# Local attention and last head attention: score products of 64 columns in two halves of the array, local scores issued ahead of the turning

## The reference, cut to what matters

```python
def _L0_xattn_ref(x, cond, Wq, bq, Wk, bk, Wv, bv, Wo, bo):   # local: 8 heads of 8 channels, window 16
    q = _pointwise(Wq, bq, x)
    k = _pointwise(Wk, bk, cond)
    v = _pointwise(Wv, bv, cond)
    k = jnp.pad(k, ((0, 0), (0, 0), (pad_left, pad_right)))
    v = jnp.pad(v, ((0, 0), (0, 0), (pad_left, pad_right)))
    idx = jnp.arange(T)[:, None] + jnp.arange(W)[None, :]
    k_win = k[:, :, idx].reshape(B, H, hd, T, W)
    v_win = v[:, :, idx].reshape(B, H, hd, T, W)
    dots = jnp.einsum('bhdt,bhdtw->bhtw', qh, k_win) * scale
    attn = jax.nn.softmax(dots, axis=-1)
    out = jnp.einsum('bhtw,bhdtw->bhdt', attn, v_win)
    return _pointwise(Wo, bo, out)
...
def _L3_xattn_ref(hidden_states, cross_attention_states, ...):   # 32 heads of 128, 8 key heads
    q, k = _rmsnorm(q, q_norm_w), _rmsnorm(k, k_norm_w)
    scores = jnp.einsum('bhqd,bhkd->bhqk', q, k) * scale + attention_mask
    probs = jax.nn.softmax(scores, axis=-1)
    out = jnp.einsum('bhqk,bhkd->bhqd', probs, v)
    return out @ Wo.T
...
x = x + jnp.tanh(g_xattn[0]) * _L0_xattn_ref(_layernorm(x), ctx_4096, ...)
x = x + jnp.tanh(g_ffn[0]) * _L0_ffn_ref(...)
...
x = x + jnp.tanh(g_xattn[3]) * _L3_xattn_ref(_layernorm(x), ctx_4096, ...)
x = x + jnp.tanh(g_ffn[3]) * _L3_ffn_ref(...)
```

## Time and profile before

| | us |
|---|---|
| median of 3 runs | 3497.05 |
| lowest and highest | 3487.21, 3498.43 |
| the profiled execution, device time | 3486.49 |
| its span, first to last instruction | 3484.5 |
| local phase, first to last band addition on DVE (63 steps) | 450.3 |
| PE busy in the whole span | 3262.8 (94%) |
| granted TensorE clock, share of full speed, whole span | 0.974 |

### The profile page before, as it was taken

How to read it: one execution, slowest core, us unless ns; L and a number is a source line. 1 busy time by engine, 2 the same in 40 slices (tenths; PEclk the granted TensorE clock), 3 DMA queues, 4 the chain that set the end, 5 groups by cost and what they waited for, 6 DMA issues and landing times. The chain is left out here.

```text
span 3484.5 us, 51177 instructions
## 1 busy us (share of the span) xinstructions
PE 3262.8 (94%) x19590; PEld 2651.0 (76%) x19590; DVE 1750.7 (50%) x3665; ACT 1461.6 (42%) x3278; POOL 1106.1 (32%) x673
## 2 busy tenths in 40 slices
PE   7777779999999999999999997999999999999997
PEld 5666655788888888888875444888788878888885
DVE  4666554333443343334344366555655565555554
ACT  4444422444444444444432354444444434444443
POOL 5444413223322322332212012334333433343332
PEclk9888879999999999999999999999999999999999
DMA  2000011111211211111101202222222222222211
GB/s 101 1 1 1 1 40 49 61 67 61 73 67 61 79 61 61 67 61 61 62 27 49 106 13 73 66 68 67 79 67 62 84 61 63 76 61 67 67 43 55
DMA packets 56549, 199.67 MB, mean 57 GB/s; under 512 B 8976, under 2 KB 9744, under 8 KB 53008
## 3 DMA queue, kind: packets, MB, share of 16 engines
q1 hardware_dynamic: 56336, 196.76, 17.1%
HBM read 192.54 MB, written 4.19 MB: 56 GB/s over the span
## 5 line engine op out<-in xcount | busy, mean ns | idle before, releaser
L1731 POOL TENSOR_TENSOR h_wol<-h_ro,h_woh 128x1024 fp32r<-128x1024 f32 x128 | 313.7, 2451 | 612.1 <-ACT h_woh L1782 612.1
L1727 POOL TENSOR_TENSOR h_wql<-h_rq,h_wqh 128x1024 fp32r<-128x1024 f32 x128 | 309.0, 2414 | 508.0 <-ACT h_wqh L1777 508.0
L2223 DVE COPY h_tf<-ps 128x512 f32<-128x512 f32 (+1 forms) x256 | 142.5, 557 | 610.9 <-PE ps L2004 610.8
L2227 DVE TENSOR_TENSOR h_ol<-ps,h_oh 128x512 fp32r<-128x512 f32 x256 | 176.9, 691 | 527.0 <-ACT h_oh L1835 526.7
L141 PE MATMUL ps<-h_woh,h_oh 128*128 128x512 f32 x1024 | 427.3, 417 | 5.7 <-DVE h_ol L2227 5.6
L141 PE MATMUL ps<-h_Xh,h_wqh 128*128 128x512 f32 x1024 | 414.3, 405 | 3.0 <-ACT h_qf L1831 1.4
L143 PE MATMUL ps<-h_woh,h_ol 128*128 128x512 f32 x1024 | 404.8, 395 | 0.0
L142 PE MATMUL ps<-h_wol,h_oh 128*128 128x512 f32 x1024 | 404.2, 395 | 0.0
L143 PE MATMUL ps<-h_Xh,h_wql 128*128 128x512 f32 x1024 | 402.2, 393 | 0.0
L142 PE MATMUL ps<-h_Xl,h_wqh 128*128 128x512 f32 x1024 | 399.9, 391 | 0.0
L1885 ACT ACTIVATE h_ex<-ps,h_mx 128x128 f32<-128x128 f32 x512 | 180.9, 366 | 270.8 <-DVE h_mx L2263 270.7
(11 more groups left out here) (292 smaller groups left out, 6351.3 us busy)
## 6 DMA issues: line engine op xcount, KB each, us to landing
h_rq<-in_L_Wq SPq DMA_DIRECT2D x128, 512.0 KB, 3.5
h_ro<-in_L_Wo SPq DMA_DIRECT2D x128, 512.0 KB, 3.5
h_rk<-in_L_Wkv SPq DMA_DIRECT2D x47, 512.0 KB, 3.7
h_craw<-in_ctxT SPq DMA_DIRECT2D x7, 1024.0 KB, 6.2
cnat<-in_ctx SPq DMA_DIRECT2D x4, 1024.0 KB, 8.3
t_craw<-in_ctxT SPq DMA_DIRECT2D x4, 1024.0 KB, 7.9
t_cn<-in_ctx SPq DMA_DIRECT2D x4, 1024.0 KB, 5.2
out_rows<-x SPq DMA_DIRECT2D x16, 256.0 KB, 2.3
```

The costliest lines, as they stand in the source:

```text
L1727: nc.gpsimd.tensor_tensor(wql[:, par], rq[:, par], f(wqh[:, par]), ALU.subtract).then_inc(m["p_wq"], 1)
L1731: nc.gpsimd.tensor_tensor(wol[:, par], ro[:, par], f(woh[:, par]), ALU.subtract).then_inc(m["p_wo"], 1)
L2223: nc.vector.tensor_copy(tf[:], ps[:, TBK, 0:PT]).then_inc(m["v_t"], 1)
L2227: nc.vector.tensor_tensor(by_head(ol), ps[:, AB, :].rearrange("p (b h t) -> p b h t", h=2, t=S), f(by_head(oh)), ALU.subtract).then_inc(m[ ...
```

## The change

Three edits. In `phase_local`, `scores(j, n)` issues for each block two products of 64 stationary columns in place of one of 128: heads 0 to 3 into PSUM partitions 0 to 63, heads 4 to 7 into 64 to 127. PE's order in a step becomes `scores(g)`, `turn(g - 2)`, extra, `values(g - 2)`. In the last tile, steps 0 to 2 get one `occupy` product in the place of the missing extra (with a wait for the last `values_out`, which frees that bank). In `phase_heads`, with `norm` alone, `scores(t)` issues two products of 64 columns for each batch in place of one of 128.

```diff
@@ -353,9 +353,11 @@
                             wait(pe, v_s, NQ * j + n)
                             for t in range(NB):
                                 t0 = (n * NB + t) * TB
-                                last = nc.tensor.matmul(
-                                    ps[:, SB_, 2 * t * KW:2 * (t + 1) * KW],
-                                    qx[:, j % 2, n * NB + t].rearrange("p h t -> p (h t)"), kp[:, j % 2, :, t0:t0 + KW], start=True, stop=True)
+                                for hh in range(2):
+                                    last = nc.tensor.matmul(
+                                        ps[S * hh:S * hh + S, SB_, 2 * t * KW:2 * (t + 1) * KW],
+                                        qx[:, j % 2, n * NB + t, HH * hh:HH * hh + HH].rearrange("p h t -> p (h t)"),
+                                        kp[:, j % 2, :, t0:t0 + KW], start=True, stop=True)
                             last.then_inc(s_s, 1)
@@ -414,9 +416,9 @@
                         for j in range(NTILE):
                             for n in range(NQ):
                                 g = NQ * j + n
+                                scores(j, n)
                                 if g >= 2:
                                     turn(g - 2)
-                                scores(j, n)
...
@@ -425,6 +427,9 @@
                                     if n == 2:
                                         value_rows(j + 1)
+                                elif n < 3:
+                                    pe.wait_ge(a_vx, NTILE)
+                                    occupy(PB + 1, 1)
                                 if n == 3 and j:
                                     output(j - 1)
@@ -1985,9 +1990,14 @@
                                 b = HB * (t % 2) + b4
-                                last = nc.tensor.matmul(ps[:, SBK, b4 * KEYS:(b4 + 1) * KEYS],
-                                                        qf[:, pair, b].rearrange("p h t -> p (h t)"), kf[:, b],
-                                                        start=True, stop=True)
+                                if norm:
+                                    for h in range(2):
+                                        last = nc.tensor.matmul(ps[S * h:S * h + S, SBK, b4 * KEYS:(b4 + 1) * KEYS],
+                                                                qf[:, pair, b, h], kf[:, b], start=True, stop=True)
+                                else:
...
```

More of the change, by code:

```diff
@@ L1987, in scores @@
                                 b = HB * (t % 2) + b4
-                                last = nc.tensor.matmul(ps[:, SBK, b4 * KEYS:(b4 + 1) * KEYS],
-                                                        qf[:, pair, b].rearrange("p h t -> p (h t)"), kf[:, b],
-                                                        start=True, stop=True)
+                                if norm:
[3 more added lines that the diff above has]
+                                else:
+                                    last = nc.tensor.matmul(ps[:, SBK, b4 * KEYS:(b4 + 1) * KEYS],
+                                                            qf[:, pair, b].rearrange("p h t -> p (h t)"), kf[:, b],
+                                                            start=True, stop=True)
                             last.then_inc(m["s_s"], 1)
```

## The result

The changed kernel takes 3358.2 us (median of 4 runs, 3353.17 to 3359.88) against 3497.05 us for the kernel before (median of 3): a ratio of 0.9608, 95% interval 0.9584 to 0.9633, or 137 us less. The forecast was 3364. All comparisons here are of fast executions; one of the kernel before (11325.11 us) and one of e10 (7994.11 us) were in the slow state and are left out. The profiled execution takes 3353.17 us, its span is 3349.7, the clock over the span 0.987.

The account below looks back on a forecast made before the run. A ring of waits through DVE, POOL and PE bounds the local phase, PE the last head attention. 3486.5 − 114 (local) − 1 − 13 (head) = 3358.5, plus half of a 10.6 gap: 3364 us, range 3325 to 3405.

Parts of the forecast that it names:

- the ring: Local phase: DVE, POOL and PE wait for one another in turn, 6.63 us a step at full clock; scores leave it.
- The step at full clock: Local phase: interval between band additions at full clock, 4.55 + 0.15 + 0.3 = 5.0 us.
- DVE's 4.55: Local phase: DVE's queued work of 4.46 us a step plus some 0.1 of gaps, the bound at full clock.
- +0.3 for POOL's holding: Local phase: POOL's masked queries hold about two DVE subtractions a tile some 0.6 us each, 0.3 us a step.
- +0.15 for PE: Local phase: in the short steps PE, not DVE, ends last, some 0.1 to 0.2 us a step on the mean.
- The clock: Local phase: share of time at half clock falls from 32% to 20% (bounds 5% and 40%), mean step 5.33 us.
- First scores and filling products: Local phase: first scores end 0.8 us sooner, −1; the three added products in the last tile cost nothing.
- Last head attention: Half-width scores save 0.10 us on PE in each of 128 steps, −13 us; bounds −4 and −23.
- More than that: Rival, 0.12: POOL and DVE hardly meet and the clock stays up; local phase 290 to 300 us, total 3318 to 3328.
- second ring: Rival, 0.11: local phase waits behind ACT's value copies; mean step 5.8 us, phase 365 us, total 3393.
- The clock stays low: Rival, 0.04: half-width products count as idle array; whole local phase at 7.2 us a step, 454 us, total 3481.
- Slower: Rival, 0.03: the two score halves do not run side by side; local step 6.2 us on PE, total 3580.

Follow-up runs that it names:

- e10: Changed kernel with two instead of four value copies per tile but the first, output not the reference's: 3348.7 us, ratio 0.958.
- e2: Kernel before with only the local scores in two half-width products, still behind the turning: 3427.8 us, ratio 0.981.
- e11: The changed kernel unaltered, run again beside e9 and e10: 3362.6 us, ratio 0.9612.
- e6: Changed kernel with two filling products in the last head attention, where PE waits for DVE's split rows at group ends: 3353.0 us, ratio 0.9602.
- e4: Changed kernel without the three filling products of the last local tile: 3358.3 us, ratio 0.9613.
- e8: Changed kernel with the row maximum of each local step taken twice on DVE, 46 us more work: 3395.6 us, ratio 0.9714.
- e5: Changed kernel with the band added in place in PSUM, so the subtraction has one SBUF input and the bank frees later: 3357.6 us, ratio 0.9614.
- e9: Changed kernel with the next scores waiting for the subtraction instead of the addition, two SBUF inputs kept: 3363.4 us, ratio 0.9624.
- e7: Changed kernel with one 0.9 us filling product on PE in each local step, ahead of the wait for the shares: 3389.0 us, ratio 0.9698.
- e12: e5 with one filling product ahead of the output product in step n = 3 of each tile but the first: 3343.0 us, ratio 0.9572.
- e3: Kernel before with only the last head attention's scores in two half-width products: 3489.3 us over 12 runs, ratio 0.9985.
- e1: Kernel before with the local scores issued ahead of the turning, still full width: 3405.6 us, ratio 0.9755.

## Why the prediction was right, point by point

**What left the ring.** As told. DVE's wait for the scores fell from 2.4 us a step to 0.15 (7.4 / 48), the additions are 5.12 us apart (5.2 to 5.5 was the sign named), the subtraction is 0.92 on the mean (near 0.9), and values product and scores each take 0.9 to 1.1 us from their start to what follows without a wait (the scores 1.03 to 1.06 where the turning comes right behind). PE's own work is 3.8 us a step in the regular tile (15.10 / 4), where 3.7 was forecast. The halves do run side by side with the same moving keys; the rival that denied it is out by e2 alone.

**The step at full clock**, forecast 5.0. Where an interval of the changed kernel was at reduced clock, the same step's interval at full clock can be taken from e11, e6, e4 or e10, which have the same tile. So put together the phase is some 313 us, 5.0 a step, as forecast (an estimate: two intervals were at full clock in none of them). The total held, but the split of it did so in part by luck. DVE's 4.55 is the base, which e8 bears out in n = 0 and n = 1. The +0.3 for POOL's holding was too large. The holding is there (23 subtractions, 0.23 us a step of DVE's time), but e5 against e9 leaves 0.08 a step of it, and at most some 0.2 by the estimate beside e9. The +0.15 for PE was then too small: e7 shows PE at the bound in n = 1 and n = 3. The two errors lie on the same path: when DVE is no longer held, it waits for PE's scores instead (0.33 us in the last row of e5), so their sum was right. What the first, the last and the six tiles with row statistics wait for was not tested.

**The clock**, the term that was mis-sized. I took 20% of the time at half clock and a price of 1 − 5.0 / 7.2 = 0.31 for each us of it: with 336 us that was 21 us. It is 44.4 of 322.8, 14%, and it costs some 10 us (322.8 − 313), 0.23 for each us. The price of 0.31 came out in e5 against e12, where nearly all falls lie behind n = 3. In the changed kernel it is less, because five of the eleven falls lie where PE does not end the step and cost next to nothing, while the six that cover the work behind n = 3 cost 1.3 to 1.7 us each. These 11 us, and 313 for 315, are the difference between −114 and −127.5. What I did not see is that a fall can also follow PE's wait behind ACT's copies in n = 3. I named PE's waits for POOL; seven of the eleven falls begin around one, but of the six that cost time four follow the wait for ACT; the other two (j = 6 and 10) begin around a wait for POOL and last 6.8 us. In the kernel of e5, where that holds for nine of twelve, one product takes all nine away.

**First scores and filling products**: the first addition stands at 27.51 in place of 26.45, in the runs behind at 26.0 to 27.7, so the −1 cannot be seen. The filling products are worth nothing (e4), as said.

**Last head attention**, forecast −13, measured −4.0 in the profile and 0.3 to 10 less by e3. The row in answer to the earlier trace rows:

```profile
2705.23 0.69 PE L1995 MATMUL ps<-h_kf,h_qf 128*64 128x64 f32 x16
2705.85 0.50 PE L141 MATMUL ps<-h_Xh,h_wqh 128*128 128x512 f32 x1
```

0.62 from the scores to the projection, inside 0.60 to 0.65. So the price of the slot was right, 0.10 a step. What failed is the count, "with 128 steps". It is saved in 103 (9.6 us). In 16 of the others, most of them at the starts and ends of groups, nothing is saved, because PE waits for something else behind the scores: in the step of [2.66 <-issue] above the same wait was 2.44 before; from the values product to the projection it is 4.77 us in both. And three falls of the clock give back 1.5 us each, 4.6 in all: two behind that wait (steps 41 and 73), one behind a wait of 1.9 us for ACT (step 65). One further step and four small ones make up the last 1.0. The sentence "what is saved on PE there is saved" is the step of the working that does not hold everywhere. That −4 was also a bound of the forecast is luck: it stood there for a dearer way out of the half width.

**The rest.** From the last addition to the first exponential of the head attention of layer 1 4.1 us are gone, which I had at 0. Before, the last 2.9 us of the half clock stretch of the earlier trace rows lie there. But the stretch is no constant: in the twelve runs behind, counted to the first scores of that attention, it takes 145 to 153 us, against 146.9 before and 142.7 in the changed kernel, so these 4 us need not be the edit's. The sum: −127.5 − 4.0 − 4.1 and +1.1 for the later first addition are −134.5, against −134.8 between the two spans.

**The rivals.** "More than that" had DVE and POOL hardly meeting, which is wrong; the phase lies between it and the forecast. The "second ring" has its wait in the trace (12 times, 15.5 us), and at full clock two copies less shorten nothing; its cost is the clock's. "The clock stays low" is out, 0.93. "Slower" is out. Three figures of the working do not come out as written, and none touches the sum: the upper end, "40% low, 5.7", is 5.0 at full clock with 5.7 as the mean of both clocks, and in "slower from about 0.17 for two halves on" the 0.17 is for one half-width product (8 x 0.17 + 0.24 − 0.81 is 0.8 us a head step, +100). The head attention's bound of −4, a way out dearer by 0.05 than the 0.10 a step, would be −6.

## What to carry to other kernels

When a wait leaves a ring, the next bound is often two engines that take turns, by step: read the interval for each kind of step at full clock, not the mean, before deciding what an edit there is worth. A short wait of PE that hides behind another engine can still cost, by the slow clock that follows it and lands on work that is on the path; a product nobody reads, put in exactly that wait, was a cheap remedy in e12. The three of e4, beside work that DVE bounds, did nothing that could be measured, and those of e7, ahead of work on the path, cost about half of their length. A saving per step counts only in the steps where that engine ends last.

## What the runs showed of the hardware

- Two fp32 products of 64 stationary columns, one in each half of the array, with the same 64 moving columns, go side by side: 32 records start to end in 1.10 to 1.15 us at full clock, about the same as the values product, whose halves have different moving columns, against 1.90 to 2.00 for 16 records of full width.
- A DVE subtraction of 512 fp32 columns with two SBUF inputs takes 0.69 us alone. In the changed kernel it takes 1.26 to 1.45 in 23 of the 27 cases in which it begins while POOL is in its masked queries (e9 has eight of 0.85); with one input from PSUM it takes 0.69 in all 64 cases, 26 of them begun beside the same POOL work. POOL is longer too where they meet: three masked queries take 3.48 us in place of 3.04, and 3.04 again in e5.
- In the last head attention a fall of the clock lasts 3.4 us, in three executions (e1, e3, e7) once 6.8. The falls came during or behind waits of PE of 1.9 to 2.7 us, and not with each of them: step 9 fell in e11 and not in the changed kernel's own profile, which is the same kernel. The kernel before has none there in its profile, while e1 has two and e2 one, and their head attention is that of the kernel before. What decides it is not shown.
- What half clock costs depends on where it falls: in the changed kernel 1.3 to 1.7 us for each fall that covers the work behind n = 3 of the local phase, and 0.2 or less for each of the five others.
